# Two feed-forward stages, the token mixer between them and the store made into one stage

## What is computed

```python
def ffn(x):                       # three blocks, the same weights in both feed-forwards
    h = layernorm_input(x)
    for blk in range(3):
        y = qlora_linear(h, 2*blk)            # 128 x 128, bias
        y = gelu(layernorm(y, gamma[blk], beta[blk]))
        y = qlora_linear(y, 2*blk + 1)
        h = y + h
    return h
x = x + ffn(layernorm(x))
s = layernorm(x); xn = s / rms(s)             # token mixer, shortcut s
u, v = silu(xn @ Wu.T + bu), silu(xn @ Wv.T + bv)
o[b] = sum(coef[lag] * v[b - lag] for lag in range(b + 1))   # over batches, per head
x = x + (u * o) @ Wo.T + bo + s
x = x + ffn(layernorm(x))
```

## Time and profile before

| | |
|---|---|
| median of 3 runs | 1644.11 us (1642.91 to 1646.92) |
| the profiled execution | 1644.81 us, its span 1642.8 us |
| mean granted TensorE clock | 0.901 |
| busy: PE, DVE | 1298.4 us (79%), 1045.8 (64%) |
| busy: ACT, POOL | 800.1 us (49%), 843.5 (51%) |
| first feed-forward | 1339.4 to 1434.1 |
| token mixer | 1434.1 to 1538.5 |
| second feed-forward | 1538.5 to 1633.0 |
| store | to 1642.8 |

### The profile page before, as it was taken

One profiled execution on the slowest core, in us unless ns is written; L12 is line 12 of the kernel. 1 busy time (PEld: TensorE's weight loads), 2 busy tenths in 40 slices (PEclk: granted clock), 3 DMA queues, 4 the chain that ended last, 5 costly groups with the idle time before them and its releaser, 6 DMA issues. The chain is left out here.

```text
span 1642.8 us, 33454 instructions
## 1 busy us (share of the span) xinstructions
PE 1298.4 (79%) x11130; PEld 837.2 (51%) x11130; DVE 1045.8 (64%) x3087; ACT 800.1 (49%) x1364; POOL 843.5 (51%) x1273
## 2 busy tenths in 40 slices
PE   4785889657988888868995588888999968766486
PEld 3664889622333333348994233333555546533364
DVE  3666545467887878735555776767766436669665
ACT  1552223213666666742331366667555547544374
POOL 3367664444335555655555676667434225365342
PEclk9986999856999999979997688889999989978798
DMA  6201232374322333133224000000000000000001
GB/s 180 50 32 53 78 82 73 81 141 105 82 66 69 84 85 85 57 104 82 78 71 122 1 1 1 2 1 1 2 2 2 2 1 1 1 0 1 1 1 52
DMA packets 86228, 79.40 MB, mean 48 GB/s; under 512 B 11711, under 2 KB 76095, under 8 KB 85760
## 3 DMA queue, kind: packets, MB, share of 16 engines
q1 hardware_dynamic: 72226, 55.07, 13.4%
q0 software_dynamic: 8640, 17.84, 3.3%
q10 hardware_dynamic: 5196, 4.35, 1.2%
HBM read 45.94 MB, written 31.28 MB: 47 GB/s over the span
## 5 line engine op out<-in xcount | busy, mean ns | idle before, releaser
L1422 ACT ACTIVATE grp_pt<-ps 128x1024 f32<-128x1024 f32 (+2 forms) x320 | 244.3, 799 | 200.9 <-PE ps L1501 122.7
L2414 DVE TENSOR_REDUCE soft_mx<-ps 128x2 f32<-128x1024 f32 (+3 forms) x256 | 201.5, 819 | 58.7 <-PE ps L2217 57.8
L2095 ACT ACTIVATE arena<-ps 128x768 f32<-128x768 f32 (+1 forms) x192 | 167.0, 881 | 98.3 <-PE ps L2250 86.4
L1022 POOL DMA_INDIRECT products<-moe_product,moe_rows_in x142 | 137.1, 965 | 121.0 <-DVE moe_product L1115 106.0
L1039 ACT ACTIVATE moe_hid<-ps 128x512 f32<-128x512 f32 x142 | 84.7, 597 | 204.5 <-PE ps L1068 203.0
L1996 POOL TENSOR_SCALAR_AFFINE_SELECT arena<-arena 128x256 f32<-128x256 f32 (+1 forms) x192 | 92.5, 485 | 145.8 <-ACT arena L2095 145.0
L1068 PE MATMUL ps<-moe_rT,moe_W_now 128*128 128x128 f32 x1136 | 157.0, 283 | 10.8 <-issue 5.1
L1521 PE MATMUL ps<-grp_pt,grp_vpad 128*32 128x160 f32 (+4 forms) x2048 | 146.9, 396 | 16.4 <-POOL grp_pt L1363 16.2
L1068 PEld LDWEIGHTS ps<-moe_rT,moe_W_now 128*128 128x128 f32 x1136 | 143.8, 198 | 13.3 <-DVE moe_rT L1107 6.7
L841 POOL DMA_INDIRECT sorted_rows<-route_row,route_target x128 | 127.6, 997 | 34.0 <-issue 30.2
L1363 POOL TENSOR_SCALAR_AFFINE_SELECT grp_pt<-grp_pt 128x256 f32<-128x256 f32 (+1 forms) x192 | 105.7, 559 | 72.6 <-ACT grp_pt L1422 71.3
(11 more groups left out here) (363 smaller groups left out, 2814.7 us busy)
## 6 DMA issues: line engine op xcount, KB each, us to landing
moe_rows_in<-sorted_rows SPq DMA_DIRECT2D x142, 65.0 KB, 1.9
route_stacks<-soft_scratch_k SPq DMA_DIRECT2D x32, 192.0 KB
arena<-products SPq DMA_DIRECT2D x8, 512.0 KB, 7.6
soft_scratch_q<-soft_parts SPq DMA_DIRECT2D x16, 192.0 KB, 2.8
route_stacks<-soft_scratch_q SPq DMA_DIRECT2D x32, 96.0 KB
arena<-products SPq DMA_DIRECT2D x4, 768.0 KB, 12.4
soft_scratch_k<-soft_parts SPq DMA_DIRECT2D x15, 192.0 KB, 2.9
products<-moe_product,moe_rows_in POOLq DMA_INDIRECT x142, 2.3
```

The costliest lines, as they stand in the source:

```text
L1022: pool.indirect_dma_start(k.products, bass.IndirectOffsetOnAxis(rows_in[:, s % RING, DEST_COL:DEST_COL + 1].bitcast(U32), 0), product[:, s ...
L1422: act.activation(at.pair(pt[:, s % 2, :], pair, seg)[:, :, 0:w], ring[(chunks_before(m) + c) % 2][:, :, 0:w], ACT.Exp, scale=scale).then_i ...
L2095: act.activation(LATENT.pair(pt[:, s % 2, :], pair, seg)[:, :, 0:w], ring[second_turn(n, c) % RING3][:, :, 0:w], ACT.Exp, scale=scale).the ...
L2414: ins = dve.tensor_reduce(mx[:, tile, half, :, r], ring[first_turn(n, d) % RING3][:, :, at:at + keys], AX.X, ALU.max)
```

## The change

`feed_forward` (both calls), `token_mixer` and `finish` go, and one stage, `tail`, takes their place. `FFN` lists 53 slots, 48 units (feed-forward, block, batch) and 5 empty ones. Batch b's mixer starts 5 slots behind its last block of the first feed-forward (`mixes`), and is spread over 8 slots. The second feed-forward's entry of a batch follows the mixer's addition. Bank 0 is shared by four uses (`in`, `out`, `turn`, `mixed`) in the order that `shared` gives; each use waits until the one before it is read. Banks 1 to 3 are `ps_y`, `ps_z` and `ps_h` have one each, `ps_uv` two instead of four. The store is one transfer of 256 KB for each batch, issued when its last addition is done. `mixed` has two buffers; a batch's taps run from the oldest lag to lag 0 over four slots. Apart from that, two `rest_part` calls in `soft_attention` move ahead of `add_back(1)`.

```diff
             add_back(0)
             stats(0)
             apply(0)
+            rest_part(0, 0)
+            rest_part(0, 1)
             add_back(1)
             stats(1)
             apply(1)
-            rest_part(0, 0)
-            rest_part(0, 1)
             add_back(2)
...
+    FFN = [(0, 0, 0), (0, 0, 1), (0, 0, 2), (0, 0, 3), (0, 0, 4), (0, 1, 0), (0, 1, 1), (0, 1, 2), (0, 1, 3), (0, 1, 4),
+           (0, 2, 0), (0, 0, 5), (0, 2, 1), (0, 0, 6), (0, 2, 2), (0, 0, 7), (0, 1, 5), (0, 2, 3), (0, 1, 6), (0, 2, 4),
+           (0, 1, 7), (0, 2, 5), None, (0, 2, 6), None, (0, 2, 7), (1, 0, 0), None, (1, 0, 1), None,
+           (1, 0, 2), (1, 1, 0), None, (1, 0, 3), (1, 1, 1), (1, 0, 4), (1, 1, 2), (1, 0, 5), (1, 2, 0), (1, 0, 6),
+           (1, 1, 3), (1, 0, 7), (1, 2, 1), (1, 1, 4), (1, 2, 2), (1, 1, 5), (1, 1, 7), (1, 1, 6), (1, 2, 3), (1, 2, 4),
+           (1, 2, 5), (1, 2, 7), (1, 2, 6)]
+    SLOTS = len(FFN)
+    assert sorted(u for u in FFN if u) == [(f, l, b) for f in range(2) for l in range(BLOCKS) for b in range(B)]
+    slot_of = {u: t for t, u in enumerate(FFN) if u}
+    units = [u for u in FFN if u]
+    unit_no = {u: i for i, u in enumerate(units)}
+    enters = {slot_of[f, 0, b]: (f, b) for f in range(2) for b in range(B)}
+    entry_no = {fb: e for e, (t, fb) in enumerate(sorted(enters.items()))}
+    leaves = {slot_of[f, BLOCKS - 1, b]: (f, b) for f in range(2) for b in range(B)}
+    mixes = {slot_of[0, BLOCKS - 1, b] + 5: b for b in range(B)}
+    FIRST, END = -4, SLOTS + 6
+
+    shared = []
+    for t in range(FIRST, END):
+        if t + 2 in enters:
+            shared.append(("in", enters[t + 2]))
+        if t - 4 in leaves:
+            shared.append(("out", leaves[t - 4]))
+        if t - 2 in mixes:
+            shared.append(("turn", mixes[t - 2]))
+        if t - 6 in mixes:
+            shared.append(("mixed", mixes[t - 6]))
+    use = {what: i + 1 for i, what in enumerate(shared)}
+    stored_first = [b for t, (f, b) in sorted(leaves.items()) if f == 1]
...
+        ps_x, ps_y, ps_z, ps_h, ps_uv = bank[0], bank[1:4], bank[4], bank[5], bank[6:8]
...
+            for b in stored_first:
+                sp.wait_ge(bank_read.sem, use["out", (1, b)])
+                sp.dma_start(ov[:, b * T:(b + 1) * T, :], k.x[:, b * T:(b + 1) * T, :]).then_inc(stored.sem, 16)
+            sp.wait_ge(stored.sem, B * 16)
...
+            for t in range(FIRST, END):
+                if unit_at(t):
+                    unit_power(unit_no[FFN[t]])
+                if t + 4 in enters:
+                    entry_power(entry_no[enters[t + 4]])
+                if t in mixes:
+                    mix_rstd_power(mixes[t])
+                if t - 1 in mixes:
+                    mix_rms_power(mixes[t - 1])
+                if t - 2 in mixes:
+                    add_shortcut(mixes[t - 2])
...
+            def silu(n):
+                need(act, gated_ready, gated_ready.at(n - 2))
+                for c in range(2 * FEAT):
+                    act.wait_ge(uv_ready.sem, uv_ready.at(n, c + 1))
+                    to = uT[:, n % 2, c, :] if c < FEAT else vT[:, c - FEAT, n, :]
+                    act.activation(to, ps_uv[c % 2], ACT.Silu, bias=k.buv[:, c:c + 1]).then_inc(silu_ready.sem, 1)
+
+            for t in range(FIRST, END):
+                if unit_at(t - 1):
+                    scale(unit_no[FFN[t - 1]])
+                if t - 4 in mixes:
+                    silu(mixes[t - 4])
+                if t + 2 in enters:
+                    copy_in(*enters[t + 2])
+                if unit_at(t - 2):
+                    gelu(unit_no[FFN[t - 2]], FFN[t - 2][1])
+                if t + 3 in enters:
+                    apply(entry_no[enters[t + 3]], enters[t + 3][1])
+                if t - 1 in mixes:
+                    apply_mix(mixes[t - 1])
+                if t - 2 in mixes:
+                    copy_xT(mixes[t - 2])
...
+            def shared_free(what):
+                need(pe, bank_read, use[what] - 1)
...
+            def second(i):
+                pe.wait_ge(gelu_ready.sem, gelu_ready.at(i))
+                need(pe, h_added, h_added.at(i - 1))
+                pe.matmul(ps_h, k.lin[:, 2 * units[i][1] + 1, :], yT[:, i % 2, :], start=True, stop=True).then_inc(second_ready.sem, 1)
...
+            def project_uv(n, c):
+                if c == 0:
+                    pe.wait_ge(bank_read.sem, use["turn", n])
+                need(pe, silu_ready, silu_ready.at(n, c - 1))
+                pe.matmul(ps_uv[c % 2], k.WuvT[:, c * P:(c + 1) * P], xT[:, n % 2, :], start=True, stop=True).then_inc(uv_ready.sem, 1)
+
+            def project_mixed(n):
+                pe.wait_ge(gated_ready.sem, gated_ready.at(n))
+                shared_free(("mixed", n))
+                pe.matmul(ps_x, k.onesb, k.bto_rows.unsqueeze(1).to_broadcast([P, T, P]), start=True, stop=True)
+                for c in range(FEAT):
+                    for j in range(T):
+                        ins = pe.matmul(ps_x[:, j * P:(j + 1) * P], gated[:, n % 2, c, j * P:(j + 1) * P], k.WtoT[:, c * P:(c + 1) * P],
+                                        start=False, stop=True, skip_group_check=True)
+                ins.then_inc(bank_set.sem, 1)
...
+            for t in range(FIRST, END):
+                if unit_at(t - 3):
+                    second(unit_no[FFN[t - 3]])
+                if t - 4 in mixes:
+                    project_uv(mixes[t - 4], 2)
+                    project_uv(mixes[t - 4], 3)
+                if unit_at(t - 2):
+                    turn_z(unit_no[FFN[t - 2]])
+                if unit_at(t + 1):
+                    first(unit_no[FFN[t + 1]])
+                if t + 2 in enters:
+                    turn_in(*enters[t + 2])
                 if t - 4 in leaves:
+                    turn_out(*leaves[t - 4])
+                if t - 2 in mixes:
+                    turn_mix(mixes[t - 2])
+                if t - 3 in mixes:
+                    project_uv(mixes[t - 3], 0)
+                    project_uv(mixes[t - 3], 1)
+                if t - 6 in mixes:
+                    project_mixed(mixes[t - 6])
...
+            def add_lag(n, lag):
+                if n < lag:
+                    return
+                dve.wait_ge(silu_ready.sem, silu_ready.at(n - lag))
+                need(dve, gated_ready, gated_ready.at(n - 2))
+                for c in range(FEAT):
+                    factor = k.coef[:, c * B + lag:c * B + lag + 1]
+                    if lag == n:
+                        ins = dve.tensor_scalar(mixed[:, n % 2, c, :], vT[:, c, 0, :], factor, None, ALU.mult)
+                    else:
+                        dve.wait_ge(taps[c].sem, counts[c])
+                        ins = dve.scalar_tensor_tensor(mixed[:, n % 2, c, :], vT[:, c, n - lag, :], factor, mixed[:, n % 2, c, :], ALU.mult, ALU.add)
+                    ins.then_inc(taps[c].sem, 1)
+                    counts[c] += 1
...
+            for t in range(FIRST, END):
+                if unit_at(t):
+                    unit_stats(unit_no[FFN[t]])
+                if t - 5 in leaves:
+                    add_x(*leaves[t - 5])
+                if t - 7 in mixes:
+                    add_mixed(mixes[t - 7])
+                if unit_at(t - 3):
+                    add_h(unit_no[FFN[t - 3]])
+                if t in mixes:
+                    mix_stats(mixes[t])
+                if t + 4 in enters:
+                    entry_stats(entry_no[enters[t + 4]], *enters[t + 4])
+                if t - 1 in mixes:
+                    norm_mix(mixes[t - 1])
+                if t - 2 in mixes:
+                    for lag in (7, 6, 5):
+                        add_lag(mixes[t - 2], lag)
+                if t - 3 in mixes:
+                    for lag in (4, 3):
+                        add_lag(mixes[t - 3], lag)
+                if t - 4 in mixes:
+                    for lag in (2, 1):
+                        add_lag(mixes[t - 4], lag)
+                if t - 5 in mixes:
+                    add_lag(mixes[t - 5], 0)
+                    gate(mixes[t - 5])
...
-STAGES = ["lin", "moe1", "soft", "moe2", "grouped", "ffn1", "toep", "ffn2"]
+STAGES = ["lin", "moe1", "soft", "moe2", "grouped", "tail"]
...
-        if "ffn1" in todo:
-            feed_forward(nc, k, "ffn1")
-        if "toep" in todo:
-            token_mixer(nc, k)
-        if "ffn2" in todo:
-            feed_forward(nc, k, "ffn2")
-        finish(nc, k, out)
+        tail(nc, k, out)
```

More of the change, by code:

```diff
@@ L2603, in copy_in @@
-            def copy_in(b):
-                act.wait_ge(turned.sem, turned.at(b))
-                act.activation(h[:, b, :], ps_x, ACT.Copy).then_inc(h_set.sem, 1)
-            def scale(u):
-                act.wait_ge(power.sem, power.at(u))
-                need(act, z_turned, z_turned.at(u - 2))
+                    ins = act.activation(entry[:, e % 2, j, :], k.x[:, b * T + j, :], ACT.Identity, bias=xshift[:, e % 2, j:j + 1],
```

(16 more changed lines are left out.)

428 lines of the change are left out of this document (172 added, 256 removed).

## The result

The changed kernel takes 1659.1 us (median of 8 runs, 1643.6 to 1672.8), the kernel before, beside it, 1643.2 (8 runs, 1641.8 to 1648.0). The ratio is 1.0075, with a 95% interval of 1.0047 to 1.0103: slightly slower. It leaves out the changed kernel's longest run, 1672.8 us, because the chip was in a slower state in it. Forecast were 1603 us, a range of 1580 to 1627, and 4 in 100 for slower. The profiled execution took 1653.4 us with a span of 1651.7, so it shows a little less than the typical loss.

What follows compares the result with a forecast made beforehand. No engine filled over 71% of three serial stages; merged, mainly VectorE would bound the mixer stretch. Terms 27.5 + 33.0 + 146 + 42.1 + 9.6 + 4.5 = 262.7 us behind 1339.4 gave 1603 us, range 1580 to 1627.

Steps and rivals of the forecast that it cites:

- Fill: Start of the new stage, to slot 4: same units, entries and order on each engine as before, 27.5 us.
- slots 4 to 15: Only feed-forward work in the new stage: 11 slots, 3 entries and one output, 33.0 us.
- slots 37 to 52: Feed-forward alone, 15 paces and 2 entries, plus 1.6 for the single banks: 42.1 us, bounds 40.5 and 46.
- drain: End of the stage to its last addition: 9.6 us against 13.6 before, bounds 8.4 and 13.6.
- store: Behind the last addition one 256 KB batch is left: 4.5 us against 10.2 before, bounds 3.4 and 10.2.
- Table loads: ScalarE, alternating Gelu and Silu: 17 loads of 1.28 us instead of 3, 14 more, 18 us.
- VectorE's sum in slots 15 to 37: VectorE's work on 17 units, 7 entries and 8 batches: 130 us, in a stretch forecast at 146 us.
- slots 24 to 36: Within slots 15 to 37: VectorE's part of the 130 us, 88 us, and the shared bank besides.
- the shared bank: Bank 0's fixed order makes VectorE wait in three places, 6 us; 28 us if its taps gave no cover.
- Lockstep: Rival: each slot costs its longest engine, so slots 15 to 37 take 165 us with the bank; 1622, chance 0.20.
- The clock rival: TensorE at 1.2 GHz in slots 15 to 37: 195 us, time 1652; decides at mean clock about 0.52; chance 0.04.
- No overlap: Rival: the bank's fixed order puts mixer and feed-forward one behind another, 28 us, within 0.3% of now; chance 0.04.

Runs made afterwards that it cites:

- e16_after_again: The changed kernel once more, unaltered, beside the kernel before: 1687.5 us, ratio 1.0107.
- e1_rest: The changed kernel with only the softmax attention reordering undone (rest_part(0, ...) behind apply(1) again): 1658.9 us, ratio 1.0084.
- e4_gelu: The changed kernel with Gelu for Silu in the mixer (another function, 1 table load instead of 17): 1642.7 us, ratio 0.9986.
- e15_best: e14_pool_bank plus reordered ScalarE scaling, TensorE products 2 and 3, and GpSimd's batch normalisation factor ahead of the entry's: 1636.8 us, ratio 0.9796.
- e17_best_gelu: e15_best with Gelu for Silu in the mixer (another function, one table load instead of 17): 1607.2 us, ratio 0.9767.
- e2_pool: The changed kernel with the mixer factor's operations (mix_rms_power) ahead of the slot's unit_power on GpSimd: 1637.5 us, ratio 0.9958.
- e13_bank_alone: The changed kernel with only a bank of its own for project_mixed, lent by the first product where batches are projected: 1662.3 us, ratio 0.9953.
- e14_pool_bank: e13_bank_alone plus the factor's operations first on GpSimd, as in e2_pool: 1637.6 us, ratio 0.9793.
- e10_y2: Control of e9_bank: e7_pool_pe_act with two banks for the first product instead of three, shared bank kept: 1672.0 us, ratio 1.0023.
- e9_bank: e7_pool_pe_act with project_mixed on a bank and counters of its own, taken from the first product's three: 1650.7 us, ratio 0.9917.
- e7_pool_pe_act: e2_pool plus project_uv 2 and 3 behind turn_z and first on TensorE, and ScalarE's second batch scaling one slot later: 1632.2 us, ratio 0.9937.

## Why the prediction was wrong

- **Fill, slots 4 to 15, slots 37 to 52, drain, store**: right to within 2.3 us each, and 117.4 us together (25.2 + 33.4 + 44.4 + 11.1 + 3.3), against 116.7 forecast. That close a sum is luck in part: in e16_after_again and e1_rest, where the stage is the same, the fill took 27.2 and 28.6 us, and the sums are 119.3 and 120.8. The single banks of `z` and `h` cost what was taken or 2.3 us more, the drain 1.5 more, the store 1.2 less. The last transfer landed 3.3 us behind the last addition, as the earlier trace rows has it.
- **Table loads**: 17 loads, right. `ACT_TABLE_LOAD` in the groups of the changed kernel:

```profile
L2712 ACT ACT_TABLE_LOAD x9 | 11.5, 1283 | 0.2
L2733 ACT ACT_TABLE_LOAD x8 | 10.3, 1283 | 1.4 <-PE ps L2808 1.2
```

 Each takes 1283 ns. The activation behind one starts 0.02 us after its end (1558.09 + 1.28, then 1559.39), so the drain of which the Trainium skill speaks ("ScalarE: Activation LUTs", What ACT_TABLE_LOAD costs) again has no place in the trace. Its advice to group by table set ("Table sets: the hidden batching unit" in the same page) is borne out in part: 16 loads fewer were worth 16 us to this kernel (e4_gelu) and 0.7 us of the stretch to e15_best (e17_best_gelu).
- **VectorE's sum in slots 15 to 37**: 130 forecast, 125.7 measured. The count was right to 4%. That e15_best takes 148.3 us in the stretch where 146 was forecast is partly luck: VectorE has 124.5 us of work, 5.5 less than the sum, and 23.8 us of waits, 7.8 more than was added.
- **The step that failed** is the term for slots 24 to 36, "VectorE's part of the 130 us" with 88 us, and 6 us for the shared bank; slots 23 to 37 took 137.2 us in the changed kernel and 100.6 in e15_best. An engine's sum is a bound only if the others' results come ahead of it, and I looked at that for the projection alone. For GpSimd I gave a batch 5.8 to 6.7 us of work, which is right (its eight operations took 6.5 us on average; the factor's five took 4.6 in the turn shown), and never asked behind what these operations are queued. The factor stands behind two waits for VectorE, VectorE's statistics behind up to 14 taps, and ScalarE's and TensorE's next units behind the factor. Undoing that in two lines gave 21 us (e1_rest 1658.9, e2_pool 1637.5) and, beside the bank, 25 us (e13_bank_alone 1662.3, e14_pool_bank 1637.6).
- **The shared bank** was mis-sized: 6 us forecast, and 28 if VectorE's taps did not cover the round trips; measured 22.4 (e10_y2 against e9_bank) and 22.7 (e16_after_again against e13_bank_alone). I let the round trip begin when VectorE adds the output and counted TensorE's product alone. In e7_pool_pe_act TensorE's wait for VectorE (5.7 us) comes before it, and the product takes 3.4 us instead of 2.2 (granted clock 0.55 from 1453.4 to 1457.3).
- **The rivals.** Lockstep (165 us) adds the longest engine of each slot and misses the same thing; 190 to 200 us is over it. The clock rival has the right time, 195 us and 1652, for a reason that is not there: it wanted a mean clock of 0.52, and the stretch was granted 0.83 with TensorE busy 112.8 of 190.2 us. In two windows of 10 us TensorE did nothing at all, and there the clock was low:

```profile
1520.00:1530.00 10.00, 0.00 (x0) 0.00 (x0) 9.90 (x29) 2.69 (x6) 9.42 (x11) 0.59 0.00 0
...
1550.00:1560.00 10.00, 0.00 (x0) 0.00 (x0) 7.74 (x11) 4.19 (x11) 6.88 (x8) 0.50 0.00 0
```

 The low clock follows the standstill, and the work behind it is slower: the four products behind the 15.4 us of rest took 3.78 us, the four ahead of it 1.88. "No overlap" came near in its result, for a part of its reason: the bank took 22 of its 28 us.
- **Chances.** The steady parts were worked out to 2 us, and the range was as narrow as if the part that was new, four in-order queues meeting in 22 slots, were known as well. A rival "an early step of a batch queued late" was missing.

What stays open: how much of the 190 us is the clock's, since no run raised it in the standstills; what the change from four banks of `ps_uv` to two costs, which no run varied (TensorE still waits 19.7 us for the Silu in e15_best); and why the changed kernel scatters over 24 us in the seven runs of its ratio where the kernel before scatters over 6 in eight. Its spans go roughly with the granted clock (1641.8 us at 0.907, 1651.7 at 0.903, 1665.5 at 0.893). That the circle hands each delay round again would explain it, but the other runs don't bear it out: e16_after_again, with the circle, and e14_pool_bank, with the factor in time, both scatter over 14 us in six runs, e15_best over 7 in five, and the kernel before over 16 in the 24 runs beside e1_rest to e4_gelu.

## What to carry to other kernels

When two stages are merged, write for each in-order queue what stands ahead of each short step, and what those steps wait for; adding up an engine's work is a forecast only after that. A step that is ready early and needed early goes ahead of anything that waits for the longest queue. A buffer that several producers fill in fixed order can cost far more than the work through it, here 22 us instead of 6: the wait begins when the producer first lacks the buffer, so look at what the reader of its last content has queued ahead.

## What the runs showed of the hardware

Short GpSimd operations can take many times their length beside VectorE. In the changed kernel one `TENSOR_SCALAR` on 128x4 elements, usually 0.24 us, took 4.75:

```profile
1519.07 4.75 POOL L2635 TENSOR_SCALAR tail_xpin<-tail_xmv 128x4 f32<-128x4 f32 x1
```

VectorE beside it, from the same execution:

```profile
1518.46 4.06 DVE L2918 SCALAR_TENSOR_TENSOR tail_mixed<-tail_vT,pack,tail_mixed 128x512 f32<-128x512 f32 x6
1522.43 1.29 DVE L2925 TENSOR_TENSOR tail_gated<-tail_mixed,tail_uT 128x512 f32<-128x512 f32 x2
1523.64 0.89 DVE L2863 BATCH_NORM_STATS2 tail_sums<-ps 128x6 f32<-128x128 f32 x4
```

It ends at 1523.82, just behind VectorE's last operation with two SBUF operands (1523.72); another of 4.74 us ends with the chain of taps and gates at 1550.6. Three of 2.59 us and one of 3.81 lie beside shorter chains of the kind. The Trainium skill ("SBUF — State Buffer", Who interferes with whom) says that a VectorE instruction with two SBUF inputs contends with a GpSimd instruction that reads SBUF. The trace agrees, and adds that the wait can last over a whole chain of such instructions, here 8. It need not: in the same execution four GpSimd operations between 1551.7 and 1555.7, beside a chain of 8 taps, took 0.4 to 1.4 us each, and why those got through is open. e15_best has two of 4.74 and 4.75 us as well, so they alone don't make the difference; in the changed kernel one of them (1545.9 to 1550.6) lay inside the turn shown above, just ahead of the late factor.
